# Four graph layers on one core: GpSimd takes over two subtractions of VectorE in the first four passes

## Chip, core and metric

The kernel runs on one core of a Trainium2 chip. The metric is the time of one launch on the device in microseconds (us). Three runs of the kernel before gave 8235.85, 8242.77 and 8251.61; the median is 8242.77.

## What is computed

12500 nodes with 64 features, 212500 edges (every node also has one to itself). Four graph layers follow one another, each added to its input and normalized over the features:

```python
x = layernorm(x + gated(x))      # 4 steps: a[dst] += W[type] @ x[src] + b[type]; x = gru(a, x)
x = layernorm(x + gin(x))        # two convolutions: mlp(x + sum of x[src])
x = layernorm(x + gcn(x))        # degree-normalized sum, relu, batch norm
x = layernorm(x + sage(x))       # edge-weighted mean
```

The change touches the first layer alone: its four steps are passes 0 to 3 of the kernel. Passes 4 to 8 are the other layers.

## The kernel before

Nodes are cut into 98 tiles of 128. A pass goes over all tiles; for each it sums the rows of the sources of that tile's edges and makes the tile's new rows. A row is kept as three bf16 parts (high, middle, low) that together carry the fp32 value, 192 numbers; TensorE works on the parts.

*How rows reach a tile.* Most edges lie in a regular grid. Ahead of the tiles, TensorE picks their source rows with one-hot matrices (L1155), ScalarE copies the result (L1423) and writes it to DRAM (bounce_f, L1436), and SyncE loads it back in another order (L771). VectorE splits these rows into parts (L1978, L1983), makes the one-hot matrices of the destinations (L1948), and TensorE sums (L1168). Edges that found no place there are left over: SyncE loads the tile's list of their source rows and own-row counts (left_recs into `lrec`, six slots, L759), GpSimd gathers the rows with four indirect DMAs a tile (L975, into a ring of six slots), VectorE makes their one-hot matrices (L1962), TensorE sums (L1190) and counts `tile_summed`.

*How a tile ends.* VectorE adds the sums to the scaled own rows (`take_sums`, L2004, counted by `sum_taken`); TensorE turns them (L1203 to L1205); ScalarE copies (L1451); TensorE multiplies by the weights (L1225 to L1227); ScalarE makes the gate (L1486); VectorE the candidate (L2084, L2087); ScalarE its tanh (L1499); VectorE the new row (L2099 to L2106, `row_made`). In pass 3 a layer norm follows (L2108 to L2046). Then the row is split: ScalarE rounds it to the high part (L1532, `hi_made`), VectorE subtracts (L2066, `rest_made`), ScalarE rounds the rest to the middle part (L1540, `mid_made`), VectorE subtracts again (L2071, `lo_part_made`), and SyncE stores the row (L786) for the next pass.

*Orders written out by hand.* All engines work in the order of their programs, and one tile's work is spread over several turns:

- VectorE, turn of tile t: sums of t-1 (L2004), rest of t-2 (L2066), grid matrix, L1978, low part of t-2 (L2071), L1962, candidate of t-1, L1983, new row of t-1. In pass 3: sums of t-1, norm of t-2, grid matrix, L1978, rest of t-2, L1962, candidate, L1983, low part of t-2, new row of t-1.
- ScalarE, turn of t: first half of L1423, middle of t-2 (L1540), L1451 of t-1, own rows of t (L1472 to L1478), gate of t-1, tanh of t-1, second half of L1423, L1436, high of t-1 (L1532). In pass 3: L1423, high of t-2, L1451 of t-1, own rows of t, gate of t-1, middle of t-2, tanh of t-1, L1423, L1436, root of t-1.
- SyncE, turn of t: waits until tile t-2 is summed; list of tile t+4 (L759), which waits until VectorE has taken the sums of tile t-2, as both use one slot; one-hot matrices (L743); bounced rows of tile t+2 (L771), which wait for L1168 of tile t; store of tile t-3 (L786), which waits for its low part.
- GpSimd, turn of T: waits for the list of T and until tile T-6 is summed; four gathers.

At a pass's end SyncE and GpSimd wait until all rows are stored.

Of the kernel before, what the change touches and what calls it, by code (L numbers as in the profile page):

```python
# [5 lines left out]
H = 64  # L6
# [4 lines left out]
NT = -(-N // P)  # L11
# [61 lines left out]
P_GIN1, P_GIN2A, P_GIN2B, P_GCN, P_SAGE = 4, 5, 6, 7, 8  # L73
# [7 lines left out]
def build(nc, x, src, dst, edge_type, edge_weight, g_W, g_b, g_w_ih, g_w_hh, g_b_ih, g_b_hh,  # L81
# [4 lines left out]
    ALU, ACT, AX = mybir.AluOpType, mybir.ActivationFunctionType, mybir.AxisListType  # L86
    ds = bass.ds
# [18 lines left out]
    xs = sb("xs", [P, NT, H], fp32)  # L106
# [175 lines left out]
    row = sb("row", [P, HID], fp32)  # L282
# [4 lines left out]
    left_over = sb("left_over", [P, HID], fp32)  # L287
    stage = sb("stage", [P, 3, 2, 3 * H], bf16)
# [83 lines left out]
    pool_ran = sem("pool_ran")  # L372
# [15 lines left out]
    lrec_landed = [sem(f"lrec_landed{i}") for i in range(6)]  # L388
# [18 lines left out]
    row_made = sem("row_made")  # L407
    hi_made = sem("hi_made")
    rest_made = sem("rest_made")
    mid_made = sem("mid_made")  # L410
# [57 lines left out]
    def lo_before(p):  # L468
        return NT * len([q for q in stores_of if q < p])

    def rows_before(p):
        return NT * len([q for q in (0, 1, 2, 3, P_GIN2B) if q < p])

    def owns_before(p):
        return NT * len([q for q in (0, 1, 2, 3, P_GIN2B, P_SAGE) if q < p])
# [116 lines left out]
    def long_loop(engine, p, first, one):  # L592

        for jj in range(first, NT):
            one(At(p, jj))
# [272 lines left out]
    def _(pool):  # L868
        g = nc.gpsimd
# [84 lines left out]
        def sum_weights(group):  # L954
# [8 lines left out]
            pool.drain()  # L963
            g.tensor_tensor(to[0:n], to[0:n], parts[0:n, 2, :], ALU.add).then_inc(weights_made, 1)

        def one_tile(at):
            if at.p == P_SAGE and at.jj > 0 and at.jj % G_TILES == 0 and at.jj // G_TILES + 1 < GROUPS:
                sum_weights(at.jj // G_TILES + 1)
            pool.wait_ge(lrec_landed[at.slot6()], at.uses6(6) * 16)
            pool.sem_inc(pool_ran, 1)  # L970
            if not (isinstance(at.i, int) and at.base < 6):
                pool.wait_ge(tile_summed, at.tiles(CREDIT_T - 5))
                pool.sem_inc(pool_ran, 1)
            for b in range(LB):
                pool.indirect_dma_start(  # L975
                    out=ring[:, at.slot6() * LB + b, 0:3 * H], out_offset=None, in_=table_of(at.p),
                    in_offset=bass.IndirectOffsetOnAxis(ap=lrec[at.slot6()][:, b, IDX:IDX + 1].bitcast(i32), axis=0)
                ).then_inc(rows_gathered[at.slot6()], 16)
# [3 lines left out]
        for p in range(NPASS):  # L982
            if p == P_SAGE:
                rest_of = squares.rearrange("p (d f) -> p d f", f=H)
                sum_weights(0)
                sum_weights(1)
                pool.wait_ge(bn_scale, 1)
                for a in range(NCH):
                    hc = hs[:, a * CH:(a + 1) * CH, :]
                    g.tensor_tensor(hc, hc, bn_gamma[:, :].rearrange("p (o f) -> p o f", o=1)  # L990
                                    .to_broadcast([P, CH, H]), ALU.mult).then_inc(ch_scaled, 1)
                for a in range(NCH + 1):
                    if a < NCH:
                        pool.wait_ge(ch_hi, a + 1)
                        at = slice(a * CH, (a + 1) * CH)
                        g.tensor_tensor(rest_of[:, at, :], xs[:, at, :], rows_now[:, at, 0:H], ALU.subtract
                                        ).then_inc(ch_rest, 1)
                    if a >= 1:
                        pool.wait_ge(ch_mid, a)
                        at = slice((a - 1) * CH, a * CH)  # L1000
                        g.tensor_tensor(rows_now[:, at, 2 * H:3 * H], rest_of[:, at, :], rows_now[:, at, H:2 * H],
                                        ALU.subtract).then_inc(ch_lo, 1)
                pool.wait_ge(sage_written, 16)
                pool.sem_inc(pool_ran, 1)
            else:
                for x3 in range(3):
                    pool.wait_ge(stored[x3], stored_before(p, x3))
                    pool.sem_inc(pool_ran, 1)
            one_tile(At(p, 0))
            long_loop(pool, p, 1, one_tile)  # L1010


    @block.tensor
# [311 lines left out]
    def _(act):  # L1325
# [186 lines left out]

        def parts(at):
            n = stores_of[at.p]
            frm = row[:, 0:n * H].rearrange("p (n f) -> p n f", n=n)
            return stage[:, at.kept(), 0:n, :], xs[:, ds(at.d(), 1), :] if at.p == 3 else frm, \
                left_over[:, 0:n * H].rearrange("p (n f) -> p n f", n=n)

        def high(at):
# [107 lines left out]
    def _(dve):  # L1627
# [428 lines left out]
        def parts(at):  # L2056
            n = stores_of[at.p]
            frm = row[:, 0:n * H].rearrange("p (n f) -> p n f", n=n)
            return stage[:, at.kept(), 0:n, :], xs[:, ds(at.d(), 1), :] if at.p == 3 else frm, left_over[:, 0:n * H].rearrange("p (n f) -> p n f", n=n), at.i * 6 + lo_before(at.p) + at.jj + 1

        def rest_of(at):
            to, frm, rest, count = parts(at)
# [10 lines left out]
        def nothing(at):  # L2073
            return

        late_parts = {p: (rest_of, low_of, nothing) for p in (0, 1, 2, P_GIN1)}
        late_parts.update({p: (normalize, rest_of, low_of) for p in (3, P_GIN2B)})
        late_parts.update({P_GIN2A: (nothing, nothing, nothing), P_GCN: (nothing, nothing, nothing),
                           P_SAGE: (normalize, nothing, nothing)})

# [14 lines left out]
        def finish(at):  # L2095
            p = at.p
            if p < P_GIN1:
                dve.wait_ge(cand_done, at.tiles(1))
                v.tensor_tensor(delta[:, :], state[at.half()][:, 0:H], cand_t[:, :], ALU.subtract)  # L2099
                dve.drain()  # L2100
                v.scalar_tensor_tensor(out=delta[:, :], in0=gate[:, H:2 * H], scalar=1.0, in1=delta[:, :],
                                       op0=ALU.add, op1=ALU.mult)
                dve.drain()
                new = dict(in0=delta[:, :], scalar=0.5, in1=cand_t[:, :], op0=ALU.mult, op1=ALU.add)
                if p < 3:
                    v.scalar_tensor_tensor(out=row[:, 0:H], **new).then_inc(row_made, 1)  # L2106
                else:
                    v.scalar_tensor_tensor(out=y[:, :], **new)  # L2108
                    dve.drain()
                    v.tensor_tensor(y[:, :], y[:, :], tile(xs, at), ALU.add)  # L2110
                    variance()
            elif p == P_GIN2B:
                dve.wait_ge(mlp_done, at.i * 6 + NT + at.jj + 1)
                v.tensor_tensor(y[:, :], mlp[:, :], tile(xs, at), ALU.add)
                variance()
            elif p == P_SAGE:
                dve.drain()
                dve.wait_ge(gate_summed, turns(at))
                v.tensor_tensor(y[:, :], ps_gate[:, 0:H], tile(xs, at), ALU.add)
                variance()  # L2120
# [248 lines left out]
```

## Time and profile before

| | |
|---|---|
| median of three runs | 8242.77 us |
| profiled execution, its span | 8249.7 us, 8247.9 us |
| busy share of PE, PEld, DVE, ACT, POOL | 76%, 66%, 82%, 46%, 62% |
| chain that ended last, by engine | DVE 43%, PE 19%, DMA 15%, DVEq 8%, issue 8%, ACT 3%, POOL 2%, SPq 2% |
| mean granted TensorE clock | 0.911 |

PE and PEld are TensorE's matmuls and weight loads, DVE is VectorE, ACT ScalarE, POOL GpSimd, SP SyncE; a q behind the name is the engine's own queue work (issuing, waiting). L975 is line 975 of the kernel before. The setup takes the span's first 1740 us; passes 0 to 3 then run until about 4771 us, passes 4 to 8 after that. The chain of waits is followed back from the last instruction, at each step to what released it.

### The profile page before, as it was taken

The page shows a single profiled execution, that of the slowest core. Times are in us where ns is not written, and L with a number is a line of the kernel's source. Part 1 is how long each engine was busy: PE and PEld are TensorE (multiplying, and loading weights), DVE is VectorE, ACT ScalarE, POOL GpSimd, SP SyncE. Part 2 cuts the span into 40 slices and gives each one's busy share as a digit, 9 for nine tenths or more (in the row PEclk, how much of TensorE's full clock was granted, in tenths as well). Part 3 has the DMA queues.
Part 4 walks back from the last instruction along what each step waited for, and adds up shares of the span by engine and source line. Part 5 has one row for each costly group of instructions (what it writes and reads, how often), then busy time and mean ns, then how long its engine had stood idle before and what let it go on. Part 6 is the DMA issues. An engine that isn't in the chain of part 4 may idle for free.

```text
span 8247.9 us, 313730 instructions
## 1 busy us (share of the span) xinstructions
PE 6295.5 (76%) x128525; PEld 5416.9 (66%) x128526; DVE 6741.0 (82%) x12922; ACT 3801.6 (46%) x11010; POOL 5075.7 (62%) x4208
## 2 busy tenths in 40 slices
PE   3676767758988887888777778866668878874887
PEld 2333333358887887888777767766667777763777
DVE  8988888858887897888789967767768977776888
ACT  1444454545444554555677743321124432224665
POOL 2454544536655665666455568867777768875665
PEclk7889988889999999999999988888889988887999
DMA  3211111258888888888777788888988888874887
GB/s 93 77 58 53 59 53 54 65 151 213 209 215 218 220 219 217 215 216 227 197 187 188 197 225 238 237 236 239 237 245 231 235 239 235 232 201 139 221 216 187
DMA packets 1129626, 1524.78 MB, mean 185 GB/s; under 512 B 377756, under 2 KB 822525, under 8 KB 1125296
## 3 DMA queue, kind: packets, MB, share of 16 engines
q1 hardware_dynamic: 888528, 874.46, 40.6%
q10 hardware_dynamic: 126656, 456.61, 16.6%
q0 software_dynamic: 113056, 174.29, 11.8%
q8 instruction: 985, 16.14, 0.8%
q14 instruction: 401, 3.28, 0.1%
HBM read 965.84 MB, written 538.99 MB: 182 GB/s over the span
## 4 chain that ended last, share of the span: by engine, by line
DVE 43%; PE 19%; DMA 15%; DVEq 8%; issue 8%; ACT 3%; POOL 2%; SPq 2%; ACTq 0%; POOLq 0%
DVE work L1983 8%; DMA work<-bounce_f 8%; DVE work L1978 6%; PE ps_agg L1168 6%; DVE work L1948 5%; DMA bounce_f<-work 4%; PE ps_pair L1155 4%; DVE work L1962 3%; DVE work L1770 2%; POOL work L975 2%; DVEq L1787 2%; DVEq L1982 2%; DVE work L1762 1%; PE ps_gate L1063 1%; PE ps_agg L1190 1%
## 5 line engine op out<-in xcount | busy, mean ns | idle before, releaser
L975 POOL DMA_INDIRECT work<-node_rows,work x3528 | 4234.6, 1200 | 2055.7 <-issue 1252.2
L1168 PE MATMUL ps_agg<-work 120*128 120x64 bf16 x42336 | 1590.7, 198 | 733.2 <-DVE work L1983 690.4
L1168 PEld LDWEIGHTS ps_agg<-work 120*128 120x128 bf16 x42336 | 1497.7, 101 | 807.7 <-issue 797.5
L1155 PE MATMUL ps_pair<-rows_now,work 128*128 128x64 bf16 x44064 | 1718.3, 199 | 272.4 <-DMA work<-src_onehots 157.2
L1155 PEld LDWEIGHTS ps_pair<-rows_now,work 128*128 128x128 fp8e4 x44064 | 1603.0, 102 | 300.8 <-issue 286.4
L1978 DVE TENSOR_TENSOR work<-work 120x1024 f32<-120x1024 f32 x882 | 1077.4, 1222 | 524.6 <-DMA work<-bounce_f 516.4
L1423 ACT ACTIVATE work<-ps_pair 120x512 f32<-120x512 f32 x1632 | 954.0, 585 | 810.4 <-PE ps_pair L1155 627.0
L1190 PE MATMUL ps_agg<-work 128*128 128x64 bf16 x27048 | 1059.8, 195 | 116.0 <-DMA work<-node_rows,work 61.4
L1983 DVE TENSOR_TENSOR work<-work 120x1024 f32<-120x1024 f32 x882 | 1080.9, 1226 | 80.9 <-issue 2.1
L1948 DVE TENSOR_TENSOR work<-iota_bf,dl_all 120x2048 bf16<-120x2048 bf16 x882 | 1075.4, 1219 | 51.9 <-issue 20.6
L1190 PEld LDWEIGHTS ps_agg<-work 128*128 128x128 bf16 x27048 | 959.9, 99 | 208.4 <-issue 116.4
L918 POOL TENSOR_SCALAR work<-work 128x36 f32<-128x36 f32 x49 | 87.9, 1794 | 841.0 <-PE ps_pair L1083 612.2
L1451 ACT ACTIVATE turned<-ps_turn 128x384 f32<-128x384 f32 (+2 forms) x784 | 317.8, 405 | 479.9 <-PE ps_turn L1205 208.7
L1962 DVE TENSOR_TENSOR work<-iota,work 128x2048 bf16<-128x2048 int16 x392 | 477.0, 1217 | 0.7 <-DMA work<-left_recs 0.7
L1389 ACT ACTIVATE work<-hs,ones_f 128x480 fp8e4<-128x480 bf16 x392 | 409.1, 1136 | 9.4 <-ACT hs L1381 5.3
L1430 ACT ACTIVATE work<-ps_pair,counts 120x64 f32<-120x64 f32 x1632 | 353.0, 328 | 31.8 <-PE ps_pair L1155 24.8
L1057 PE MATMUL ps_agg<-hs,above 128*128 128x384 bf16 x882 | 203.9, 401 | 157.7 <-DVE hs L1762 157.7
L1762 DVE TENSOR_TENSOR work<-iota,work 128x6912 bf16<-128x6912 int16 x147 | 317.6, 2160 | 4.3 <-issue 1.2
L1478 ACT ACTIVATE agg_sb<-hs,work 128x64 f32<-128x64 f32 x1176 | 309.3, 336 | 0.0
L1074 PE MATMUL ps_agg<-hs,stage 128*25 128x384 bf16 x882 | 240.1, 453 | 82.0 <-DVE stage L1824 82.0
L920 POOL TENSOR_SCALAR work<-hs 128x36 f32<-128x36 f32 x196 | 296.9, 1569 | 0.0
L1511 ACT ACTIVATE std<-moments,epsilon 128x1 f32<-128x1 f32 x294 | 86.6, 295 | 439.2 <-DVE moments L2036 437.0
(342 smaller groups left out, 9955.0 us busy)
## 6 DMA issues: line engine op xcount, KB each, us to landing
bounce_f<-work ACTq DMA_DIRECT2D x918, 480.0 KB
work<-bounce_f SPq DMA_DIRECT2D x882, 480.0 KB
work<-src_onehots SPq DMA_DIRECT2D x918, 256.0 KB
work<-node_rows,work POOLq DMA_INDIRECT x3528
hs<-grid_vals SPq DMA_DIRECT2D x49, 960.0 KB, 4.9
node_rows<-stage SPq DMA_DIRECT2D x686, 48.0 KB
rows_now<-node_rows SPq DMA_DIRECT2D x42, 768.0 KB, 8.0
src_onehots<-work SPq DMA_DIRECT2D x17, 1536.0 KB, 8.5
```

What stands on the lines that cost most here:

```text
L975: pool.indirect_dma_start(out=ring[:, at.slot6() * LB + b, 0:3 * H], out_offset=None, in_=table_of(at.p), in_offset=bass.IndirectOffsetOnA ...
L1155: last = mm(to[:, a * H:(a + 1) * H], oh[s.buf()][:, EIGHT * m + a, :], rows_now[:, s.chunk() * CHUNK + EIGHT * m + a, x * H:(x + 1) * H], ...
L1168: last = mm(acc[:, to:to + H], hot, tops(thirds[at.two()])[0:ROWS, x, b, :], start=x == 0 and (b == 0 or p < P_GIN1 and b == GB // 2), sto ...
L1190: last = mm(acc[:, to:to + n], ohs[:, h * P:(h + 1) * P], ring[:, u * LB + b, x * H:x * H + n], start=False, stop=end and x == 2 and closes)
L1389: last = a_(oh_tiles[:, :, :, j + t, k, :], lo_tiles[:, t, :, :, k * SB:(k + 1) * SB].rearrange("p u i b -> p i b u"), ACT.Relu, bias=ones ...
L1423: a_(to, frm, ACT.Copy).then_inc(pair_copied, 1)
L1430: last = a_(to[:, a, :], frm[:, a, :], ACT.Copy, scale=weight_f[s.group() % 2][0:ROWS, col:col + 1])
L1762: return v.tensor_tensor(to.rearrange("p n (h o) -> p n h o", o=2), iota512[:, 0:width].rearrange("p (g h o) -> p g h o", g=1, o=2) .to_br ...
L1948: last = v.tensor_tensor(to, numbers(ROWS, GB), spread(dl_all[0:ROWS, ds(at.d(more), 1), :].rearrange("p o n -> p (o n)"), ROWS, GB), ALU. ...
L1962: v.tensor_tensor(halves(hots, LB), iota512[:, :].rearrange("p (g h o) -> p g h o", g=1, o=2) .to_broadcast([P, LB, K * P // 2, 2]), pair_ ...
L1978: v.tensor_tensor(x[:, 1, :, :], x[:, 0, :, :], tops(x)[:, 0, :, :], ALU.subtract)
L1983: v.tensor_tensor(x[:, 2, :, :], x[:, 1, :, :], tops(x)[:, 1, :, :], ALU.subtract).then_inc(parts_made, 1)
```

## The change

GpSimd makes both subtractions of the split in passes 0 to 3. In its turn of tile T, in front of the gathers, it splits tile T-7 (passes 0 to 2) or T-8 (pass 3); the last seven or eight tiles of a pass are split behind the last gathers. Its wait for the list now stands behind the split. `row` and `left_over`, 128 columns wide, are used as two buffers of 64 in passes 0 to 2 (`left_over` in pass 3 too), and VectorE waits, before it writes a row, for the rest of two tiles before. ScalarE's lines stay where they are and read the new places.

```diff
+    def split_views(at):
+        half = slice(at.half() * H, at.half() * H + H)
+        frm = xs[:, ds(at.d(), 1), :] if at.p == 3 else row[:, half].rearrange("p (n f) -> p n f", n=1)
+        return stage[:, at.kept(), 0:1, :], frm, left_over[:, half].rearrange("p (n f) -> p n f", n=1)
...
@@ GpSimd
+        def split_row(at):
+            to, frm, rest = split_views(at)
+            count = lo_before(at.p) + at.jj + 1
+            pool.wait_ge(hi_made, count)
+            pool.sem_inc(pool_ran, 1)
+            g.tensor_tensor(rest, frm, to[:, :, 0:H], ALU.subtract).then_inc(rest_made, 1)
+            pool.wait_ge(mid_made, count)
+            pool.sem_inc(pool_ran, 1)
+            g.tensor_tensor(to[:, :, 2 * H:3 * H], rest, to[:, :, H:2 * H], ALU.subtract).then_inc(lo_part_made, 1)
+
+        def split_behind(p):
+            return 7 if p < 3 else 8
+
         def one_tile(at):
...
-            pool.wait_ge(lrec_landed[at.slot6()], at.uses6(6) * 16)
-            pool.sem_inc(pool_ran, 1)
             if not (isinstance(at.i, int) and at.base < 6):
                 pool.wait_ge(tile_summed, at.tiles(CREDIT_T - 5))
                 pool.sem_inc(pool_ran, 1)
+            if at.p < P_GIN1 and at.jj >= split_behind(at.p):
+                split_row(At(at.p, at.jj - split_behind(at.p)))
+            pool.wait_ge(lrec_landed[at.slot6()], at.uses6(6) * 16)
+            pool.sem_inc(pool_ran, 1)
             for b in range(LB):
...
             long_loop(pool, p, 1, one_tile)
+            if p < P_GIN1:
+                for jj in range(NT - split_behind(p), NT):
+                    split_row(At(p, jj))
...
@@ ScalarE, parts
+            if at.p < P_GIN1:
+                return split_views(at)
...
@@ VectorE
-        late_parts = {p: (rest_of, low_of, nothing) for p in (0, 1, 2, P_GIN1)}
-        late_parts.update({p: (normalize, rest_of, low_of) for p in (3, P_GIN2B)})
+        late_parts = {p: (nothing, nothing, nothing) for p in (0, 1, 2)}
+        late_parts.update({P_GIN1: (rest_of, low_of, nothing), 3: (normalize, nothing, nothing),
+                           P_GIN2B: (normalize, rest_of, low_of)})
...
                 if p < 3:
-                    v.scalar_tensor_tensor(out=row[:, 0:H], **new).then_inc(row_made, 1)
+                    if not (isinstance(at.i, int) and at.base < 2):
+                        dve.wait_ge(rest_made, at.i * 6 + lo_before(p) + at.jj - 1)
+                    v.scalar_tensor_tensor(out=row[:, at.half() * H:(at.half() + 1) * H], **new).then_inc(row_made, 1)
```

## Rows read from the trace of the kernel before

**Rows 1.** One line of VectorE, passes 0 to 3; count: min/median/max ns, first to last start.

```profile
L2004 DVE TENSOR_TENSOR agg_sb<-agg_sb,ps_agg x98: 403/409/422, 1781.4 to 2497.1; 128x256 f32<-128x256 f32 x98
L2004 DVE TENSOR_TENSOR agg_sb<-agg_sb,ps_agg x98: 410/414/422, 2531.7 to 3218.8; 128x256 f32<-128x256 f32 x98
L2004 DVE TENSOR_TENSOR agg_sb<-agg_sb,ps_agg x98: 410/414/422, 3254.1 to 3943.4; 128x256 f32<-128x256 f32 x98
L2004 DVE TENSOR_TENSOR agg_sb<-agg_sb,ps_agg x98: 420/420/423, 3975.7 to 4770.7; 128x256 f32<-128x256 f32 x98
```

**Rows 2.** Chain of waits, pass 1 (2465 to 3175), share by line.

```profile
by line: DVE work L1983 13.3%; DVE work L1978 10.1%; DVE work L1962 9.9%; issue 9.9%; DVE work L1948 9.3%; PE ps_agg L1168 7.5%; PE ps_pair L1155 5.3%; DMA work<-bounce_f 4.7%; PE ps_agg L1190 3.2%; DMA bounce_f<-work 2.7%; PE ps_gate L1225
```

**Rows 3.** Groups by line, GpSimd, pass 1, then pass 3: busy us, mean ns | idle before.

```profile
L975 POOL DMA_INDIRECT work<-node_rows,work x387 | 446.0, 1153 | 265.4 <-issue 155.1 <-DMA work<-left_recs 110.3
L975 POOL DMA_INDIRECT work<-node_rows,work x359 | 394.0, 1098 | 356.5 <-DMA work<-left_recs 216.3 <-issue 139.3 <-PE ps_agg L1190 0.9
```

**Rows 4.** Two lines counted from about 2500 on, columns as in Rows 1.

```profile
L1540 ACT ACTIVATE stage<-left_over x49: 243/246/258, 2505.2 to 2866.7; 128x64 bf16<-128x64 f32 x49
L975 POOL DMA_INDIRECT work<-node_rows,work x217: 942/966/2012, 2510.3 to 2875.2; - x109
```

**Rows 5.** Timeline, pass 1: start us, us, engine line op [idle before <-releaser].

```profile
2866.10 0.24 ACT L1532 ACTIVATE stage<-row 128x64 bf16<-128x64 f32 x1
...
2866.37 0.23 DVE L2066 TENSOR_TENSOR left_over<-row,stage 128x64 f32<-128x64 f32 x1
2866.51 1.22 DVE L1948 TENSOR_TENSOR work<-iota_bf,dl_all 120x2048 bf16<-120x2048 bf16 x1
...
2866.72 0.25 ACT L1540 ACTIVATE stage<-left_over 128x64 bf16<-128x64 f32 x1
...
2867.31 0.49 ACT L1451 ACTIVATE turned<-ps_turn 128x384 f32<-128x384 f32 x1 [0.34 <-PE ps_turn L1205]
...
2869.24 0.28 ACT L1486 ACTIVATE gate<-ps_gate 128x128 f32<-128x128 f32 x1 [0.25 <-PE ps_gate L1227]
...
2869.51 0.40 SPq L759 DMA_DIRECT2D work<-left_recs  x1
...
2870.06 0.21 DVE L2084 SCALAR_TENSOR_TENSOR cand<-gate,ps_gate 128x64 f32<-128x64 f32 x1
...
2872.81 0.24 ACT L1532 ACTIVATE stage<-row 128x64 bf16<-128x64 f32 x1
...
2873.00 0.95 POOL L975 DMA_INDIRECT work<-node_rows,work  x1 [0.30 <-issue]
...
2874.96 0.52 SPq L759 DMA_DIRECT2D work<-left_recs  x1
...
2875.19 1.21 POOL L975 DMA_INDIRECT work<-node_rows,work  x1 [1.24 <-DMA work<-left_recs]
...
2881.70 1.41 POOL L975 DMA_INDIRECT work<-node_rows,work  x1 [1.04 <-DMA work<-left_recs]
```

**Rows 6.** Timeline, pass 3.

```profile
4301.78 0.25 ACT L1540 ACTIVATE stage<-left_over 128x64 bf16<-128x64 f32 x1
...
4302.62 0.26 ACT L1499 ACTIVATE cand_t<-cand 128x64 f32<-128x64 f32 x1 [0.59 <-DVE cand L2087]
...
4303.95 0.22 DVE L2099 TENSOR_TENSOR delta<-state,cand_t 128x64 f32<-128x64 f32 x1
...
4305.55 0.42 DVE L2004 TENSOR_TENSOR agg_sb<-agg_sb,ps_agg 128x256 f32<-128x256 f32 x1
...
4306.79 0.33 SPq L759 DMA_DIRECT2D work<-left_recs  x1
...
4312.02 0.94 POOL L975 DMA_INDIRECT work<-node_rows,work  x1 [2.06 <-DMA work<-left_recs]
```

**Rows 7.** Two GpSimd lines, whole span: min/median/max ns, first and last start.

```profile
L932 POOL TENSOR_TENSOR work<-work x49: 192/3710/3790, 157.7 to 1698.4; 128x4 f32<-128x4 f32 x49
L964 POOL TENSOR_TENSOR counts<-counts,typed_v x17: 365/501/1070, 7417.6 to 8162.1; 120x96 f32<-120x96 f32 x16, 40x96 f32<-40x96 f32 x1
```

More of the change, by code:

```diff
@@ L1514, in parts @@
             n = stores_of[at.p]
+            if at.p < P_GIN1:
+                return split_views(at)
             frm = row[:, 0:n * H].rearrange("p (n f) -> p n f", n=n)
-            return stage[:, at.kept(), 0:n, :], xs[:, ds(at.d(), 1), :] if at.p == 3 else frm, \
+            return stage[:, at.kept(), 0:n, :], frm, \
                 left_over[:, 0:n * H].rearrange("p (n f) -> p n f", n=n)
@@ L2058, in parts @@
             frm = row[:, 0:n * H].rearrange("p (n f) -> p n f", n=n)
-            return stage[:, at.kept(), 0:n, :], xs[:, ds(at.d(), 1), :] if at.p == 3 else frm, left_over[:, 0:n * H].rearrange("p (n f) -> p n f", n=n), at.i * 6 + lo_before(at.p) + at.jj + 1
+            return stage[:, at.kept(), 0:n, :], frm, left_over[:, 0:n * H].rearrange("p (n f) -> p n f", n=n), at.i * 6 + lo_before(at.p) + at.jj + 1
         def rest_of(at):
```

## Prediction

> **What bounds the kernel now.** A tile is a block of 128 nodes; the change touches the four passes 0 to 3, 98 tiles each. I first divided time by tiles: the line that takes a tile's sums (L2004) starts 98 times in each pass, and first to last start give 7.38, 7.08, 7.11 and 8.20 us a tile [rows 1]. Then the chain of waits, cut to pass 1: VectorE's four wide lines L1983, L1978, L1962 and L1948 lead it, TensorE's L1168 and L1155 stand behind [rows 2]. So VectorE mostly sets the pace, and taking work from it looks right. Third, the engine that is to get the work: per tile GpSimd issues four gathers of 1.15 us with 0.30 us between, 5.8 us of 7.1, and the rest is a wait for left_recs, the tile's list of row numbers [rows 3].
>
> The fourth reading decides: which tile each engine is at. Counting starts in pass 1, the L1540 at 2866.72 belongs to tile 47 (49 in the window, the first from pass 0) and the gather at 2875.19 is the 217th, so the first of tile 54 [rows 4, 5]. The new order puts tile 47's split in front of tile 54's gathers, behind tile 53's. These end at 2873.95; ScalarE uses tile 47's rest at 2866.72 [rows 5]. GpSimd would come 7.2 us late, a whole tile. It has idle time, but at the wrong moment, and the reason is its wait for the list.
>
> **The change part by part.**
>
> *Off VectorE: two subtractions a tile.* L2066 starts at 2866.37 and the next line at 2866.51 [rows 5]: neighbours overlap, so it costs 0.14 us in the stream, and I take the same for its twin L2071. Where VectorE is the bound that is at most 0.28 x 392 = 110 us; where it waits, nothing. I take nothing, as it will wait for others (below).
>
> *Onto GpSimd: the same two, of 128x64.* No row has this form there. Below stands L932, 4 columns, 0.19 us at its shortest; above L964, 96 columns, 0.37 us [rows 7]. I take 0.3, nearer to L964 in width, and 0.1 for the handing over. If VectorE's work gets in the way the price is larger: beside VectorE's wide instructions in the setup, the L932 of 0.19 us has a median of 3.71 us [rows 7]. *The Trainium skill ("SBUF — State Buffer", section "Who interferes with whom") says why: a VectorE instruction with two SBUF inputs and a GpSimd one that reads SBUF exclude each other for its whole length; the rows agree, and by the rule alone the time would be the second rival's.* In the order that I expect, ScalarE is held up before the gate, so VectorE has run out of work (at L2084, in pass 3 at L2099) while GpSimd subtracts; I charge no such wait there.
>
> *Onto GpSimd: two waits with a ScalarE step between.* Queued behind them are the four gathers. Alone they would fit: 5.8 + 0.3 + 0.3 + about 0.4 for L1540 and two handovers = 6.8 us, under 7.1.
>
> *On ScalarE: the wait of L1540 is now for GpSimd.* The engine works in order, and behind L1540 stand the copy of the turned sums (L1451), the scaling of own rows, the gate (L1486), the tanh, the second copy of pairs and the issue of the bounce write. All of VectorE's and TensorE's tail hangs on these. This wait closes a ring, for passes 0 to 2:
>
> 1. Rest of tile T-8 ready, to row T-7 made and its high part done. From L1540 at 2866.72 to the next L1532's end at 2873.05: 6.33. In it 0.34 is L1451's wait for the turn, and 0.54 lies between the end of the gate (2869.52) and L2084 (2870.06), when VectorE still did grid work; both vanish when ScalarE is the late one: 5.45.
> 2. Tile T-6's sums are taken by VectorE at the same moment, since finish(T-7) and take_sums(T-6) are neighbours. SyncE may overwrite that tile's slot only then: from the end of L1532 to L759 it is 3.17 (2866.34 to 2869.51) and 1.91 (2873.05 to 2874.96), as the loads and stores in front in its queue allow. I take 2.3.
> 3. L759 to the first gather: 5.68 (to 2875.19) and 6.74 (to 2881.70), the list landing behind a 480 KB load in the same queue. I take 5.8, as the DMA will have more room.
> 4. Four gathers of tile T: 4 x 1.15 + 3 x 0.30 = 5.5 [rows 3].
> 5. Then, in front of the gathers of T+1, the first subtraction of tile T-6: 0.4.
>
> Sum 5.45 + 2.3 + 5.8 + 5.5 + 0.4 = 19.5 us, all legs but the noted ones from rows 5. It leads from the split of tile T-8 to that of tile T-6, two tiles: **9.7 us a tile** against 7.38, 7.08 and 7.11. Today the ring is open: VectorE makes the rest without asking whether the gathers have been issued.
>
> A pass's first seven slots have no split in front, and its last seven splits come behind all gathers, so I count 90 slow intervals: 90 x (3 x 9.7 - 21.57) = 680 us.
>
> *Pass 3 splits tile T-8, not T-7, in front of tile T's gathers.* ScalarE's L1540 now stands behind the gate and before the tanh (L1499), so the ring is one tile long: the subtraction of T-8 lets L1540 and L1499 of T-7 run (from the overlapped start, 0.5); VectorE from L2099 to the end of L2004, tile T-6's sums, 2.02; L2004 to L759, 0.82; L759 to the gathers of T, 5.23 [rows 6]; gathers 4 x 1.10 + 0.9 = 5.3 [rows 3]; subtraction 0.4. Sum 14.3. SyncE also has the store of tile T-8 in front of that L759, and it waits for the second subtraction; that comes about 0.8 after the first, well before tile T-6's sums, and hides there. Since the load and the store that now delay L759 will be out early, I take 13.6: 90 x (13.6 - 8.20) = 490 us.
>
> *Two buffers for row and rest.* VectorE's write of a new row waits for the rest of two tiles before, made one GpSimd slot earlier in the ring: nothing. Without the second buffer the wait would be in the ring.
>
> *Waits swapped on GpSimd* (credit of tile_summed before the list): the credit is long there when the list lands, nothing in passes 0 to 2. In pass 3 it allows the split before the list, without which the ring would not turn at all.
>
> Sum: 680 + 490 = 1170. The profiled execution took 8249.7 (span 8247.9 and 1.8 around it), 7 above the median of 8242.8. Forecast 8249.7 + 1170 - 7 = about 9410 us.
>
> **Own range of this forecast.** Passes 0 to 2: 8.7 a tile if the gathers come 4.5 after L759 and leg 2 is 1.5; 10.6 if leg 1 keeps its 6.33 and leg 2 is 3.17. Pass 3: 14.3 as summed, 12.8 if L759 follows the sums at once and the gathers come 4.5 after it. That is 90 x (3 x 8.7 - 21.57 + 4.6) = 820 to 90 x (3 x 10.6 - 21.57 + 6.1) = 1470: 9060 to 9710. The two low figures, 1.5 and 4.5, are estimates a little under the shortest rows (1.91 and 5.23), since a slower pace empties the queues.
>
> **Rivals.**
>
> *It gets faster: GpSimd's idle time is enough.* VectorE is rid of 0.28 us a tile, its chain in rows 2 shortens, GpSimd's 6.8 fits under 7.1. For: VectorE leads the chain, and GpSimd idles 265 us in pass 1 [rows 3]. Against: that idling lies before the list's landing, after the time when the rest is wanted. It decides from one point: the gathers of T-1 must be issued when tile T-7's high part is ready; today they end 7.6 later (2873.95 against 2866.34). Time: 8242.8 - 110 = 8130, 8190 if half the tiles wait for the gate as now.
>
> *GpSimd is the bound by its own work, not by the ring.* If lists came early enough to hide, a tile would cost GpSimd 6.8 and twice a wait for VectorE's wide instructions. These fill 4 x 1.22 of about 7.1 us, so a wait of 0.69 x 0.61 = 0.4 on the mean and 1.2 at most. 7.6 a tile costs 90 x (0.2 + 0.5 + 0.5) = 110 us, nothing in pass 3: 8350. At the full 1.2 it is 9.2 and 9.0: 90 x (1.8 + 2.1 + 2.1 + 0.8) = 610: 8850. *This is the Trainium skill's rule named above at work.* For: the medians of L932. Against: L759 stands behind VectorE's sums in all rows 5 and 6, so the lists cannot come early.
>
> *No change*: the gain on VectorE and GpSimd's lateness would have to cancel; only chance speaks for it. 8240.
>
> **How the numbers follow.** The ring 0.87; GpSimd's own work 0.07 (8350 to 8850); faster 0.04; no change 0.02. The time is the ring's, 9410. The range 8830 to 9760 holds 0.93 of the ring and a little of the second rival, some 0.8. A difference of 0.2% (16 us) is what a measurement can tell here: faster 0.04, within 0.03, slower 0.93.
>
> **What would show it.** Right: passes 0 to 2 some 9 to 10 us a tile between starts of L2004, pass 3 more, 12 to 14.6; ScalarE idle before L1540, released by GpSimd's new subtraction, several us a tile; VectorE idle before L2084 (passes 0 to 2) and L2099 (pass 3), share of busy time down; GpSimd still waiting for left_recs in front of its gathers; passes 4 to 8 as before. New subtractions of about 0.3 us would say that VectorE's ports were free, of 1 us and more that the second rival has a part. Wrong: GpSimd's subtraction starting within 1 us of L1532, or no wait for left_recs left in passes 0 to 3.

## The result, and the profile after

The changed kernel took 9582.57 us, the median of four runs (9568.94 to 9596.81); the kernel before took 8244.53 beside it (four runs, 8235.85 to 8251.61). The ratio is 1.163, 95% interval 1.160 to 1.166: slower by a sixth. The prediction was 9410, range 8830 to 9760. The profiled execution's span is 9595.0 us, its mean granted TensorE clock 0.848.

Lines below the GpSimd part have moved: L2004 is now L2029, L759 L764, L771 L776, L786 L791, L975 L995, L1532 L1557, L1540 L1565, L1168 L1191, L1190 L1213, L1225 to L1227 L1248 to L1250. GpSimd's subtractions are L976 (rest) and L979 (low part).

First the pace. The line that takes a tile's sums, passes 0 to 3 in turn; it answers to [rows 1]:

```profile
L2029 DVE TENSOR_TENSOR agg_sb<-agg_sb,ps_agg x98: 407/411/422, 1789.1 to 2798.8; 128x256 f32<-128x256 f32 x98
L2029 DVE TENSOR_TENSOR agg_sb<-agg_sb,ps_agg x98: 412/414/422, 2828.7 to 3825.0; 128x256 f32<-128x256 f32 x98
L2029 DVE TENSOR_TENSOR agg_sb<-agg_sb,ps_agg x98: 410/414/422, 3857.8 to 4853.9; 128x256 f32<-128x256 f32 x98
L2029 DVE TENSOR_TENSOR agg_sb<-agg_sb,ps_agg x98: 419/421/422, 4885.7 to 6110.4; 128x256 f32<-128x256 f32 x98
```

Over 97 intervals that is 10.41, 10.27, 10.27 and 12.63 us a tile, where it was 7.38, 7.08, 7.11 and 8.20. The increases, times 97, are 294, 309, 307 and 430 us, 1340 in all; the span grew by 1347. Passes 4 to 8 keep their time to within 8 us.

Then who is waited for. The chain of waits of pass 1 (2828 to 3825), for [rows 2], and the groups of GpSimd in pass 1, for [rows 3]:

```profile
by line: POOL work L995 22.0%; DMA work<-left_recs 20.0%; issue 12.7%; PE ps_agg L1213 11.4%; PE ps_agg L1191 7.2%; PE ps_gate L1248 5.8%; PE ps_pair L1178 3.8%; PE ps_gate L1250 3.1%; PE ps_gate L1249 3.1%; SPq L791 2.8%; ACT turned L1474 
```

```profile
L995 POOL DMA_INDIRECT work<-node_rows,work x381 | 433.8, 1139 | 355.5 <-DMA work<-left_recs 248.7 <-issue 106.8
L976 POOL TENSOR_TENSOR left_over<-row,stage 128x64 f32<-128x64 f32 x96 | 61.6, 642 | 46.5 <-ACT stage L1557 45.6
L979 POOL TENSOR_TENSOR stage<-left_over,stage 128x64 bf16<-128x64 f32 x96 | 52.5, 547 | 44.8 <-ACT stage L1565 44.3 <-DMA work<-left_recs 0.5
```

VectorE's wide lines, which led [rows 2], are gone from the head: gathers and their lists lead. GpSimd has more work than before and yet waits longer for lists (248.7 us against 110.3): so its work does not look like the bound here, its place in a ring does; the experiments test that. ScalarE's L1565 waited 344.8 us for L976 in this pass.

The timeline of pass 1 shows one round of that ring, from tile 10's rest to tile 12's:

```profile
2953.05 0.31 POOL L976 TENSOR_TENSOR left_over<-row,stage 128x64 f32<-128x64 f32 x1
...
2953.39 0.26 ACT L1565 ACTIVATE stage<-left_over 128x64 bf16<-128x64 f32 x1 [6.50 <-POOL left_over L976]
...
2954.08 1.22 PE L1248 MATMUL ps_gate<-state_w,turned 69*128 69x256 f32 x2 [6.03 <-ACT turned L1474]
...
2956.62 0.28 ACT L1509 ACTIVATE gate<-ps_gate 128x128 f32<-128x128 f32 x1 [1.40 <-PE ps_gate L1250]
...
2956.93 0.22 DVE L2110 SCALAR_TENSOR_TENSOR cand<-gate,ps_gate 128x64 f32<-128x64 f32 x1 [7.22 <-ACT gate L1509]
...
2959.41 0.41 DVE L2029 TENSOR_TENSOR agg_sb<-agg_sb,ps_agg 128x256 f32<-128x256 f32 x1
...
2959.69 0.24 ACT L1557 ACTIVATE stage<-row 128x64 bf16<-128x64 f32 x1
...
2960.11 1.01 POOL L976 TENSOR_TENSOR left_over<-row,stage 128x64 f32<-128x64 f32 x1 [0.54 <-ACT stage L1557]
...
2962.19 0.70 PE L1248 MATMUL ps_gate<-state_w,turned 69*128 69x256 f32 x2
...
2962.39 0.33 SPq L764 DMA_DIRECT2D work<-left_recs  x1
...
2968.14 1.76 POOL L995 DMA_INDIRECT work<-node_rows,work  x1 [5.76 <-DMA work<-left_recs]
...
2972.69 0.94 POOL L995 DMA_INDIRECT work<-node_rows,work  x1 [0.30 <-issue]
...
2973.66 0.31 POOL L976 TENSOR_TENSOR left_over<-row,stage 128x64 f32<-128x64 f32 x1
...
2974.00 0.26 ACT L1565 ACTIVATE stage<-left_over 128x64 bf16<-128x64 f32 x1 [6.62 <-POOL left_over L976]
```

Tile 10's middle part starts at 2953.39; tile 11's high part ends at 2959.93 (leg 1, 6.54); tile 12's sums are taken at the same time, and its slot's new list, tile 18's, is issued at 2962.39 (leg 2, 2.46); the first gather starts 5.75 later (leg 3), the fourth ends at 2973.63 (leg 4, 5.49), and tile 12's middle part starts 0.37 after that (leg 5). Sum 20.61 us for two tiles. Only every second tile waits: tile 11's L976 at 2960.11 follows its L1557 by 0.18, and the intervals between starts of L2029 alternate between about 7 and 13.5 us. So the ring runs through the even tiles; the odd ones have slack.

Pass 3, for [rows 6], one round for one tile:

```profile
5406.24 0.33 SPq L764 DMA_DIRECT2D work<-left_recs  x1
...
5409.04 1.45 POOL L995 DMA_INDIRECT work<-node_rows,work  x1 [4.53 <-DMA work<-left_recs]
...
5414.91 0.94 POOL L995 DMA_INDIRECT work<-node_rows,work  x1 [0.30 <-issue]
5415.86 0.32 POOL L976 TENSOR_TENSOR left_over<-xs,stage 128x64 f32<-128x64 f32 x1
5416.21 0.26 ACT L1565 ACTIVATE stage<-left_over 128x64 bf16<-128x64 f32 x1 [5.56 <-POOL left_over L976]
5416.38 0.24 ACT L1522 ACTIVATE cand_t<-cand 128x64 f32<-128x64 f32 x1
...
5416.65 0.23 DVE L2125 TENSOR_TENSOR delta<-state,cand_t 128x64 f32<-128x64 f32 x1 [4.11 <-ACT cand_t L1522]
...
5418.25 0.42 DVE L2029 TENSOR_TENSOR agg_sb<-agg_sb,ps_agg 128x256 f32<-128x256 f32 x1
5418.77 0.33 SPq L764 DMA_DIRECT2D work<-left_recs  x1
```

Between the two L764 lie 12.53 us: list to gather 2.80, gathers 6.81 (with one long pause of 1.35), subtraction to the middle part's start 0.36, from there over the tanh to the end of the sums 2.46, and 0.10 to the next list.

### The profile page after: what moved, and what is told of

Read it like the earlier page. It is cut to its first block, busy times and chain, and to the rows that moved or that the text cites. A ratio compares the mean times of both kernels' runs of the same rounds, so it can differ in the third digit from the quotient of the medians.

```text
span 9595.0 us, 314514 instructions
## 1 busy us (share of the span) xinstructions
PE 6730.7 (70%) x128525; PEld 5813.8 (61%) x128526; DVE 6672.3 (70%) x12138; ACT 3816.5 (40%) x11010; POOL 5487.9 (57%) x4992
## 4 chain that ended last, share of the span: by engine, by line
PE 22%; DVE 21%; DMA 21%; POOL 14%; issue 11%; DVEq 6%; ACT 3%; SPq 3%; POOLq 0%; ACTq 0%
POOL work L995 13%; DMA work<-left_recs 9%; DMA work<-bounce_f 6%; PE ps_agg L1191 5%; PE ps_agg L1213 4%; DVE work L2008 3%; PE ps_pair L1178 3%; DMA bounce_f<-work 3%; DVE work L2003 2%; DVE work L1795 2%; PE ps_gate L1248 2%; DVEq L1812 2%; PE ps_agg L1080 2%; DVEq L2007 1%; PE ps_gate L1086 1%
## 5 line engine op out<-in xcount | busy, mean ns | idle before, releaser
L995 POOL DMA_INDIRECT work<-node_rows,work x3528 | 4240.4, 1202 | 2565.4 <-DMA work<-left_recs 1448.7
L1191 PE MATMUL ps_agg<-work 120*128 120x64 bf16 x42336 | 1580.6, 198 | 519.1 <-DVE work L2008 503.5
L1178 PE MATMUL ps_pair<-rows_now,work 128*128 128x64 bf16 x44064 | 1760.7, 201 | 240.0 <-DMA work<-src_onehots 163.2
L1191 PEld LDWEIGHTS ps_agg<-work 120*128 120x128 bf16 x42336 | 1492.5, 101 | 572.8 <-issue 565.8
L1178 PEld LDWEIGHTS ps_pair<-rows_now,work 128*128 128x128 fp8e4 x44064 | 1651.0, 104 | 266.4 <-issue 250.3
L1213 PE MATMUL ps_agg<-work 128*128 128x64 bf16 x27048 | 1223.3, 208 | 110.9 <-DMA work<-node_rows,work 102.0
L1213 PEld LDWEIGHTS ps_agg<-work 128*128 128x128 bf16 x27048 | 1138.5, 109 | 218.2 <-issue 139.5
L1248 PE MATMUL ps_gate<-state_w,turned 69*128 69x256 f32 x784 | 393.2, 596 | 853.5 <-ACT turned L1474 852.5
L2110 DVE SCALAR_TENSOR_TENSOR cand<-gate,ps_gate 128x64 f32<-128x64 f32 x392 | 86.5, 221 | 1127.7 <-ACT gate L1509 1124.8
L1565 ACT ACTIVATE stage<-left_over 128x64 bf16<-128x64 f32 (+1 forms) x588 | 155.4, 264 | 1646.3 <-POOL left_over L976 1558.2
L1248 PEld LDWEIGHTS ps_gate<-state_w,turned 69*128 69x128 f32 x784 | 165.5, 263 | 878.2 <-ACT turned L1474 876.4
L1226 PE MATMUL ps_turn<-eye,agg_sb 128*128 128x128 f32 x392 | 131.6, 336 | 404.6 <-DVE agg_sb L2029 403.4
L2125 DVE TENSOR_TENSOR delta<-state,cand_t 128x64 f32<-128x64 f32 x392 | 86.3, 220 | 394.4 <-ACT cand_t L1522 394.4
```

The lines of the kernel that those rows point to most:

```text
L995: pool.indirect_dma_start(out=ring[:, at.slot6() * LB + b, 0:3 * H], out_offset=None, in_=table_of(at.p), in_offset=bass.IndirectOffsetOnA ...
L1178: last = mm(to[:, a * H:(a + 1) * H], oh[s.buf()][:, EIGHT * m + a, :], rows_now[:, s.chunk() * CHUNK + EIGHT * m + a, x * H:(x + 1) * H], ...
L1191: last = mm(acc[:, to:to + H], hot, tops(thirds[at.two()])[0:ROWS, x, b, :], start=x == 0 and (b == 0 or p < P_GIN1 and b == GB // 2), sto ...
L1213: last = mm(acc[:, to:to + n], ohs[:, h * P:(h + 1) * P], ring[:, u * LB + b, x * H:x * H + n], start=False, stop=end and x == 2 and closes)
L1248: mm(ps_gate[:, 0:4 * H], turned[0:H + 1 + K, 2 * P:3 * P], state_w[:, :], start=True, stop=False)
```

## The experiments

Theory: the ring. Rival: GpSimd's own work, made dearer beside VectorE's instructions. All ratios are to the kernel before, run beside them.

**1. Pass 3 split one tile later in the order.**

```diff
-            return 7 if p < 3 else 8
+            return 7
```

> The changed kernel, but pass 3 too splits tile T-7 (not T-8) in front of tile T's gathers. Ring theory: the ring of pass 3 then spans two tiles. From the changed kernel's trace: middle part to sums taken 2.5, list issued 0.6, landed 3.2, gathers begin 0.8, last 5.4, subtraction 0.4, sum 12.9, so 6.5 a tile, under the 8.2 of before: pass 3 returns to 8.2 to 8.6 a tile, passes 0 to 2 stay at 10.3: 9200 us (9150 to 9250). Theory of GpSimd's own work (gathers and subtractions are too much for it): the same work per tile, so pass 3 stays at 12.6 and the time at 9580.

9246.62 us, ratio 1.122 (1.120 to 1.125). Pass 3 fell from 12.63 to 9.09 us a tile: most of its loss was the one-tile ring. It didn't come back to 8.20, and GpSimd's groups of pass 3 say why:

```profile
L995 POOL DMA_INDIRECT work<-node_rows,work x375 | 530.5, 1415 | 146.6 <-issue 118.8 <-DMA work<-left_recs 27.9
L976 POOL TENSOR_TENSOR left_over<-xs,stage 128x64 f32<-128x64 f32 x96 | 93.2, 971 | 17.8 <-ACT stage L1557 16.2
L979 POOL TENSOR_TENSOR stage<-left_over,stage 128x64 bf16<-128x64 f32 x96 | 38.4, 400 | 54.6 <-ACT stage L1565 52.3 <-DMA work<-left_recs 2.3
```

Work and idle add up to 881 of 882 us, and only 27.9 is spent waiting for lists any more: where the ring opens, the rival takes over. Gathers take 1.42 us on the mean, where they took 1.11 in pass 3 of the change, and L976 0.97, where it took 0.35.

**2. One tile less everywhere.**

```diff
-            return 7 if p < 3 else 8
+            return 6 if p < 3 else 7
```

> The changed kernel, but passes 0 to 2 split tile T-6 and pass 3 tile T-7 in front of tile T's gathers: the same instructions, one tile earlier. Ring theory: the ring of passes 0 to 2 spans three tiles instead of two, 20.7/3 = 6.9 a tile, and no longer bounds; what is left is GpSimd's own 6.8 and its waits for VectorE's instructions, 7.1 to 7.8 a tile: 8250 to 8500 us. Theory of GpSimd's own work: nothing changes in passes 0 to 2, 10.3 a tile, 9580 us (9200 if pass 3 alone gains).

8540.51 us, ratio 1.037 (1.035 to 1.038); 7.59, 7.95, 8.01 and 9.09 a tile. The split is the same work on the same engine, one slot earlier, and 1042 of 1338 us are gone. That is the ring's share. The time is a little over the expected band of 8250 to 8500, and in pass 1 GpSimd's time is again filled by its gathers, the pauses between them, and the split with its short waits for ScalarE (477.8 + 107.3 + 47.2 + 20.2 + 69.6 + 45.2 = 767 of 771 us), with no wait for lists:

```profile
L995 POOL DMA_INDIRECT work<-node_rows,work x377 | 477.8, 1267 | 107.3 <-issue 103.3 <-PE ps_agg L1213 0.3
L979 POOL TENSOR_TENSOR stage<-left_over,stage 128x64 bf16<-128x64 f32 x96 | 69.6, 725 | 45.2 <-ACT stage L1565 45.2
L976 POOL TENSOR_TENSOR left_over<-row,stage 128x64 f32<-128x64 f32 x96 | 47.2, 492 | 20.2 <-ACT stage L1557 18.8
```

**3. The list sooner.** SyncE issues a list ahead of the bounced rows and the store, in the turn before; the lists at the ends of a pass move with it.

```diff
-            if not (known and at.jj + 4 >= NT):
-                load_recs(at, 4)
...
             if has_step(at):
...
+            if not (known and at.jj + 5 >= NT):
+                load_recs(at, 5)
...
             if not (known and at.jj + 2 >= NT):
                 load_msgs(at, 2)
```

> The changed kernel, but SyncE issues a tile's list ahead of the bounced rows' load and of the row store of the turn before, instead of behind them. Split and gathers stay as they are. Ring theory: the leg from sums taken to list issued falls from 2.7 to some 0.3, the landing, no longer behind 480 KB, from 4.3 to some 3.2: 3.5 less in a ring of two tiles, 1.7 a tile in passes 0 to 2; in pass 3 (one tile) the landing alone, some 0.8: 9582 - 90 x (3 x 1.7 + 0.8) = 9050 us (8900 to 9250). Theory of GpSimd's own work: the list is not the bound, 9580. Theory that the port shared with VectorE is the cost: 9580 too.

9193.09 us, ratio 1.114 (1.112 to 1.117): 389 us off the change, in the expected range, though 530 was the figure. Leg 2 fell to nothing (in passes 1 and 2 the list is issued 0.1 us after the sums, where it was 2.75), the list landed about 0.4 sooner in the even tiles, and in pass 1 the gathers took 6.2 on the mean where they took 5.5; in passes 0 to 2 the pace is 8.63, 9.08 and 9.18.

**4. The split left out.** The kernel before without VectorE's two subtractions; ScalarE still makes the middle part, from zeros, and no longer waits for the rest.

```diff
             to, frm, rest, count = parts(at)
+            if at.p < P_GIN1:
+                return
...
```

> The kernel before with VectorE's two subtractions left out in passes 0 to 3 and put nowhere else (middle and low parts of the rows are then not computed). It measures what taking them from VectorE can bring at most. By 0.14 us each in VectorE's stream: 110 us if VectorE is the bound throughout, 8130; I expect half, as the gate's path through TensorE and ScalarE stands close behind: 8190 us (8130 to 8240). If the rival that VectorE's relief is worth much were right: under 8100.

8251.32 us, ratio 1.000 (0.999 to 1.001): a miss. With both subtractions gone from VectorE and added nowhere, nothing was gained in all. GpSimd in pass 1:

```profile
L977 POOL DMA_INDIRECT work<-node_rows,work x377 | 564.1, 1496 | 114.9 <-issue 111.0 <-DMA work<-left_recs 4.0
```

The same gathers took 1.50 us instead of 1.15 [rows 3]; 679 of 694 us are gathers and the pauses between them. So GpSimd became the bound of that pass. It isn't that VectorE did more: its busy share fell from 0.88 to 0.83. What changed is the order on it. With L2071 gone from between them, three wide lines follow one another without a break, and the gathers that start in the first and the last of these took 1.81 and 1.87 us on the mean, where they took 1.19 and 1.01. The pace of passes 1 and 2 rose a little (7.08 and 7.11 to 7.15 and 7.19 a tile); in pass 3, where GpSimd still waited 128.9 us for lists, it fell from 8.20 to 7.99.

**5. and 6. Zeros instead of subtractions**, in the changed kernel (5) and in that of experiment 2 (6).

```diff
-            g.tensor_tensor(rest, frm, to[:, :, 0:H], ALU.subtract).then_inc(rest_made, 1)
+            g.memset(rest, 0.0).then_inc(rest_made, 1)
...
-            g.tensor_tensor(to[:, :, 2 * H:3 * H], rest, to[:, :, H:2 * H], ALU.subtract).then_inc(lo_part_made, 1)
+            g.memset(to[:, :, 2 * H:3 * H], 0.0).then_inc(lo_part_made, 1)
```

> The changed kernel, but GpSimd writes zeros where it subtracted (same two outputs, same waits and counts; rest and low part are then not computed). A writing instruction reads nothing, so it does not compete with VectorE's two-input instructions for reads. Port theory (the ring came out longer than forecast because the subtractions wait for VectorE): the leg from last gather to middle part falls from 0.95 to 0.3 and the leg from there to the next row loses some 0.4, as VectorE is not held up: 0.5 a tile in passes 0 to 2, little in pass 3: 9410 us (9350 to 9480). Without a port effect only the shorter instruction counts, 0.15 us once in two tiles: 9560.

9534.35 us, ratio 1.155 (1.153 to 1.158): a miss. I had taken leg 5 from its mean over all tiles (0.9). In the even tiles, which carry the ring, L976 starts when VectorE has run dry and takes 0.31 to 0.32; the long ones (1.01 at 2960.11, beside VectorE's wide lines) are in the odd tiles, off the ring. There L1565 now came sooner, and ScalarE then waited for TensorE's turn of the sums, 0.63 us against 0.23 in the change (a row of experiment 5's timeline):

```profile
2957.70 0.49 ACT L1474 ACTIVATE turned<-ps_turn 128x384 f32<-128x384 f32 x1 [0.63 <-PE ps_turn L1228]
```

> The kernel e2_one_tile_less, with zeros written instead of the two subtractions. There the ring is loose and GpSimd's own work sets 7.6 to 8.0 a tile in passes 0 to 2, of which the subtractions have medians of 0.46 and 0.78 us against 0.30 at the shortest. Port theory: both fall to some 0.2: 0.8 less a tile in passes 1 and 2, 0.5 in pass 0, which ends at the pace of before: 8540 - 190 = 8350 us (8290 to 8420), what is left being pass 3. Ring theory alone (no port): 8540 less 0.2 x 270 = 8490.

8394.16 us, ratio 1.017 (1.015 to 1.019), 146 us under experiment 2. With the ring open GpSimd's own work is the path, and here the longer subtractions count: in pass 1 the writes took 0.15 to 0.17 us on the mean beside the same VectorE lines, the subtractions 0.49 and 0.73. Some 0.3 of these 0.9 us a tile is that a write is also shorter by itself (0.15 against 0.30 at the shortest); the rest is what subtractions lose beside VectorE. *The Trainium skill ("SBUF — State Buffer", section "Who interferes with whom") has a VectorE instruction with two SBUF inputs exclude a GpSimd one that reads SBUF, and not one that only writes it; these rows agree.*

**7. and 8. Three gathers a tile**, the fourth batch of left-over rows not fetched, without the split (7) and in the kernel before (8). TensorE's count of gathers to wait for changes with it.

```diff
-            for b in range(LB):
+            for b in range(LB - 1 if at.p < P_GIN1 else LB):
...
```

> e4_no_split with three gathers a tile instead of four in passes 0 to 3 (the fourth batch of left-over rows is not fetched there). e4 gained nothing; its gathers take 7.0 us a tile in passes 1 and 2, against 5.6 before, so GpSimd may have become its bound. If so, a gather less lets VectorE's relief show: 8130 us (8060 to 8180), 60 to 110 under e8_three_gathers. If instead the path over TensorE and ScalarE to the gate bounds both, it equals e8_three_gathers within 20 us.

8149.24 us, ratio 0.987 (0.984 to 0.989).

> The kernel before with three gathers a tile in passes 0 to 3, the control for e7_no_split_three_gathers. GpSimd idles there before each list, so it is no bound: 8220 us (8180 to 8250), whatever theory holds for e4.

8201.84 us, ratio 0.994 (0.992 to 0.996). With a gather less on GpSimd, leaving the split out is worth 53 us (8201.84 − 8149.24); with four it was worth nothing. So VectorE's gain exists, of the size of half the 110 us that the prediction named as its most, but GpSimd stands in front of it.

**9. and 10. TensorE kept busy**, in the changed kernel (9) and in that of experiment 5 (10).

```diff
+            if prev is not None and at.p < 3 and at.jj % 2 == 0 and at.jj >= 8:
+                for _ in range(8):
+                    mm(ps_gate[:, 4 * H:8 * H], eye[0:H + 1 + K, :], state_w[:, :], start=True, stop=True)
             if prev is not None:
                 first_product(prev)
```

What led to it is the granted clock in the round shown above: the even tile's stall, its gate products, and the odd tile after it. Columns of these windows of the changed kernel: length, busy time of PE, PEld, DVE, ACT and POOL, granted clock, DMA share, GB/s:

```profile
2950.00:2952.00 2.00, 0.00 (x0) 0.00 (x0) 0.00 (x0) 0.00 (x0) 1.47 (x2) 1.00 1.07 269
2952.00:2953.50 1.50, 0.00 (x0) 0.00 (x0) 0.00 (x0) 0.11 (x1) 1.26 (x2) 0.54 0.15 43
2953.50:2955.00 1.50, 0.92 (x2) 0.84 (x3) 0.00 (x0) 1.50 (x8) 0.74 (x2) 0.50 0.25 33
2955.00:2956.70 1.70, 1.70 (x11) 1.44 (x11) 0.00 (x0) 0.30 (x2) 1.40 (x2) 0.50 0.16 37
2959.00:2961.00 2.00, 2.00 (x73) 2.00 (x71) 1.93 (x5) 0.98 (x3) 1.46 (x2) 1.00 0.84 225
```

> What is open is leg 1, which took 6.12 us on the mean of pass 1 where 5.45 was summed, and takes two values in turn, near 5.5 and 6.54. In the tile with the long stall TensorE's three gate products (L1248 to L1250) take 1.22, 0.85 and 0.85 us with the granted clock at 0.50, in the next tile 0.70, 0.49 and 0.49 at 1.00. Here TensorE makes eight products of eye and state_w (0.53 us each, into columns of ps_gate that nobody reads) in every second tile of passes 0 to 2, while it would stand idle for 6 us ahead of the gate products. If the idle time ahead of the gate products is what lets the clock fall: leg 1 in those tiles 5.4 instead of 6.54, 0.55 us a tile less, 9.7 a tile, 150 us in all: 9430 us (9390 to 9480). If leg 1 is long for another reason, the bounced rows or VectorE: 9580, or above, by up to 4.3 us of products in every second tile that the stall doesn't hide.

9651.37 us, ratio 1.169 (1.165 to 1.174): slower, a miss as a whole. It falls apart by pass. In pass 0 the clock was held in most even tiles (of the 87 tiles 8 to 94 it was low at the gate products of 14, of 43 in the change), as in these rows of its timeline:

```profile
2103.35 3.70 PE L1296 MATMUL ps_gate<-state_w,eye 69*128 69x256 f32 x16
2109.37 0.70 PE L1248 MATMUL ps_gate<-state_w,turned 69*128 69x256 f32 x2 [2.31 <-ACT turned L1477]
```

There leg 1 fell from 6.55 to 5.88 on the mean of the even tiles and the round of the ring from 21.03 to 20.54. The even tiles fall into two groups: of the 42 from tile 8 to 90, the 30 whose clock was held had a leg 1 of 5.41 at the median (5.61 on the mean), the 12 others 6.52 on the mean. In the second half of pass 1 and in most of pass 2 the stall left the even tiles: the intervals between sums, 7.8 and 12.4 in turn, became 10 to 12 throughout, the eight products stood in tiles that had no stall (leg 1 up to 9.85), and a round took 21.0 to 21.2 on the mean of these passes.

> The kernel of the run before this one, and GpSimd writes zeros in place of its two subtractions (the middle and low parts of rows are not computed). With writes alone the time fell by 48 us where 170 were expected: in the tile without a stall L1565 came 0.9 us earlier, and ScalarE then waited 0.63 us for TensorE's turn of the sums (L1228). If TensorE's low clock in the tile before is why that turn is late, both savings add up: 150 and 120 us off the change's 9583, so 9310 us (9280 to 9350). If the turn is late at the full clock too, the writes save no more than they did: 9385.

9629.17 us, ratio 1.166 (1.163 to 1.169): it failed in the same way (10.14, 10.48 and 10.59 a tile), so passes 1 and 2 say nothing on the two savings. In pass 0, where the stall kept to the even tiles, the change's 10.41 became 10.27 in experiment 9, 10.18 in experiment 5 and 10.14 with both: there the savings of 0.14 and 0.23 do not add up.

**11. The list sooner in the kernel before**, the edit of experiment 3.

> The kernel before with the list of a tile issued by SyncE ahead of the bounced rows and the store, the edit that took 390 us off the change. If the list is worth this only inside the ring, the kernel before, where nothing but the gathers hangs on the list, keeps its time: 8245 us (8225 to 8265), with less waiting for left_recs on GpSimd (771 us before). If an early list is worth something by itself, so that part of the 390 us had nothing to do with the ring: 8100 to 8200.

8242.07 us, ratio 0.999 (0.997 to 1.001). GpSimd's wait for lists fell from 110.3 to 81.9 us in pass 1 and nobody gained by it: the 389 us of experiment 3 are a leg of the ring, not something that early lists are worth by themselves.

## Why the prediction was right, and where its sizes were off

The mechanism held at each point that was named: the two-tile ring in passes 0 to 2 and the one-tile ring in pass 3, ScalarE waiting for L976, VectorE standing before L2110 (7.22 us) and L2125 (4.11), GpSimd still waiting for lists, TensorE's and VectorE's shares down from 76% and 82% to 70%. Experiment 2 opens the ring without taking work away and gets 1042 us back; experiments 3 and 11 show that the list is a leg of it. The legs, even tiles of pass 1 (mean of 41 rounds, worked out from the timeline's rows):

| leg | predicted | measured |
|---|---|---|
| 1, rest to next row's high part | 5.45 | 6.56 |
| 2, to L764 | 2.3 | 2.67 |
| 3, to the first gather | 5.8 | 5.19 |
| 4, four gathers | 5.5 | 5.87 |
| 5, subtraction of tile T-6 | 0.4 | 0.37 |
| sum, two tiles | 19.5 | 20.67 |

- *Leg 1.* "Both vanish when ScalarE is the late one: 5.45" is true of the two waits that it struck out, and left a third out: with the stall TensorE stands idle for 6 us, its granted clock goes from 1.00 to 0.50 (2.4 to 1.2 GHz), and the gate products take 1.22, 0.85 and 0.85 us instead of 0.70, 0.49 and 0.49. In the 130 tiles of passes 0 to 2 (of tiles 8 to 94) where they were slow, leg 1 was 6.55 on the mean; in the 131 others 5.7 to 5.9 by pass, at its shortest 5.39. Leg 1 is 1.1 of the 1.2 that the sum was short, and experiment 9 ties it to the clock: with the clock held, the even tiles of pass 0 come out at 5.41 at the median, the predicted size.
- *Legs 2 to 4* are off by 0.4, −0.6 and 0.4, and nearly cancel.
- *Leg 5.* The subtraction takes 0.31 to 0.32 in the ring, as VectorE has run out of work there; 0.3 was predicted. Beside the wide instructions it takes up to 1.36, in odd tiles, which have slack.
- *"A pass's first seven slots have no split in front, ... so I count 90 slow intervals"*: wrong in its first half. Those slots are on GpSimd, and the first split stands behind seven tiles' gathers. In pass 1 these start at 2811.72 and the first L976 comes at 2850.45, 12.9 us after row 0's high part. The first seven intervals of a pass took 19, 27, 26 and 35 us more than before, 107 in all, where the prediction had nothing.
- *Pass 3*, "I take 13.6": the pace of the last 90 intervals is 12.58, an increase of 395 us and not 490. L764 followed the sums at once (0.10 at the median, 0.59 on the mean, 0.82 predicted), and "L759 to the gathers, 5.23" measured 3.24 + 0.78 = 4.02, with the DMA engines' share down from 0.77 to 0.48. The low end that the prediction gave for this pass, 12.8, rests on the same two causes; the measured pace is a little under it.

So 838 + 395 + 107 = 1340 stand against 680 + 490 = 1170. That the sum came this close is in part luck: 158 and 107 were missing, and pass 3's 95 too many made up for some of it. The prediction also took each round as two like tiles; that only the even ones wait was not in it.

- *Off VectorE, nothing*: right as a number for the change. Experiments 4, 7 and 8 add that with four gathers a tile it would have been nothing without the ring too, for a reason that the prediction didn't have: GpSimd.
- *The second rival* (7.6 to 9.2 a tile, 8350 to 8850) is real, and lay behind the ring: 7.6 to 8.0 in passes 0 to 2 of experiment 2, and 8540 us. "Nothing in pass 3" was its wrong part; there it costs 0.9 a tile.

What stays open: what the low clock costs the change in all. Pass 0 of experiment 9 returned 0.49 us a round; the other passes didn't test it. Nor did a run ask why the stall changed its tiles in passes 1 and 2, or why gathers in experiment 4 came to start where they take longest.

## What to carry to other kernels

Before work is moved to an idle engine, count which tile each engine is at when the result is wanted: on an engine that works in order, a new wait puts all that stands behind it into a ring with whatever feeds it, and one slot more or less decided 1042 us here. Then write the ring's legs down, ask of every engine that will stand idle in it what it does on waking, and count the first round of each pass by the engine that comes late, not by the slots that the edit touches. An engine with a third of its time idle can still be the next bound, if relief elsewhere makes its own instructions longer.

## What the runs showed of the hardware

*A gather on GpSimd takes longer beside VectorE's wide instructions.* It is an indirect DMA, not arithmetic, yet of the 348 gathers of tiles 10 to 96 in pass 1 of the kernel before, the 58 that started while VectorE was idle took 0.94 or 0.95 us each, the 44 that started in L1978 1.52 on the mean and up to 2.01. Not every one does: those that started in L1962 took 1.01 on the mean. In the changed kernel's timeline, GpSimd's gathers and then VectorE's wide instructions, which end at 2949.7:

```profile
2946.72 1.55 POOL L995 DMA_INDIRECT work<-node_rows,work  x1 [4.83 <-DMA work<-left_recs]
2948.58 1.95 POOL L995 DMA_INDIRECT work<-node_rows,work  x1 [0.31 <-issue]
2950.83 0.94 POOL L995 DMA_INDIRECT work<-node_rows,work  x1 [0.30 <-issue]
2952.08 0.94 POOL L995 DMA_INDIRECT work<-node_rows,work  x1 [0.30 <-issue]
```

```profile
2946.22 1.22 DVE L1973 TENSOR_TENSOR work<-iota_bf,dl_all 120x2048 bf16<-120x2048 bf16 x1
2947.36 1.22 DVE L2003 TENSOR_TENSOR work<-work 120x1024 f32<-120x1024 f32 x1
2948.49 1.22 DVE L1987 TENSOR_TENSOR work<-iota,work 128x2048 bf16<-128x2048 int16 x1
```

This goes with experiment 4's result: 0.35 us more for each of four gathers in pass 1 is 1.4 us a tile, far more than the 0.28 taken from VectorE, and with one gather less (experiments 7 and 8) the gain shows.

*A stall can cost again when it ends.* In the round shown, TensorE had stood idle for 6.03 us when the gate products started; the granted clock was then at 0.50 (1.2 GHz), where it had been at 1.00 (2.4 GHz), and these products, on the path, took 1.1 us longer than in a tile without the stall, on top of the stall itself.
